# First attention of a two-layer network on one core: the order of an iteration's pieces, their PSUM places, the row sums and the kept queries are changed

## The reference, cut to what matters

```python
x = layer_norm(ctx); lat = layer_norm(layernorm(x))
q = lat @ Wq                                # 512 x 1024 for a batch
kv = concatenate([x, lat], axis=1) @ Wkv    # 32 + 512 keys and values
dots = einsum('bhid,bhjd->bhij', q, k) * scale
attn = softmax(dots, axis=-1)
out = einsum('bhij,bhjd->bhid', attn, v) ... @ Wout
x = x + out
# then: a routed feed-forward (8 experts, best one), a second attention over the
# context alone, and a second routed feed-forward (8 experts, best two)
```

## Time and profile before

| what | value |
|---|---|
| median of 3 runs | 803.49 us (798.53, 803.49, 803.7) |
| the profiled execution's own time | 803.94 us |
| its span, first to last instruction | 802.2 us |
| mean granted TensorE clock | 0.94 |
| PE busy | 705.0 us, 88% of the span, 4966 matmuls |
| PEld busy | 451.9 us, 56% |
| DVE busy | 473.4 us, 59% |
| ACT busy | 384.8 us, 48% |
| POOL busy | 378.6 us, 47% |
| chain that ended last | PE 74%, issue 8%, DVE 7%, ACT 4%, POOL 3%, DMA 2% |

### The profile page before, as it was taken

The page is one execution under the profiler, slowest core; times in us unless marked ns, Lnnn a source line. Parts: engine busy times, 40 slices in busy tenths (PEclk is TensorE's granted clock), DMA queues, the critical chain, the costliest instruction groups (busy, mean ns, idle before and its releaser), DMA issues.

```text
span 802.2 us, 14393 instructions
## 1 busy us (share of the span) xinstructions
PE 705.0 (88%) x4966; PEld 451.9 (56%) x4966; DVE 473.4 (59%) x950; ACT 384.8 (48%) x572; POOL 378.6 (47%) x369
## 2 busy tenths in 40 slices
PE   4999999999999999999999999986993777468871
PEld 4554555555555545555545455486993443458771
DVE  4646484595594875676675666653444287634443
ACT  4465554554654563654554643353661543235450
POOL 7164463563563574464365454524334126745542
PEclk9999999999999999999999999998997697569996
DMA  9999999950000000000030003302205200213215
GB/s 252 199 203 200 205 170 5 4 2 1 1 1 2 4 11 1 1 1 2 1 119 1 1 1 107 119 17 57 58 25 170 54 1 31 64 46 82 74 55 177
DMA packets 109869, 50.64 MB, mean 63 GB/s; under 512 B 44804, under 2 KB 103048, under 8 KB 109800
## 3 DMA queue, kind: packets, MB, share of 16 engines
q1 hardware_dynamic: 106280, 42.46, 35.7%
q0 software_dynamic: 3520, 7.27, 2.6%
HBM read 20.07 MB, written 29.64 MB: 62 GB/s over the span
## 4 chain that ended last, share of the span: by engine, by line
PE 74%; issue 8%; DVE 7%; ACT 4%; POOL 3%; DMA 2%; SPq 1%; another core or an unknown queue 1%; ACTq 0%; POOLq 0%; DVEq 0%
PE PSUM L1583 14%; PE PSUM L1615 13%; PE PSUM L1436 9%; PE PSUM L1550 5%; PE PSUM L1452 3%; PE PSUM L1681 3%; PE PSUM L1399 3%; PE PSUM L1400 3%; PE PSUM L1401 3%; PE PSUM L1564 2%; PE PSUM L1557 2%; PE PSUM L1601 2%; PE PSUM L1645 2%; PE PSUM L1395 1%; PE PSUM L1765 1%
## 5 line engine op out<-in xcount | busy, mean ns | idle before, releaser
L852 ACT ACTIVATE PT<-PSUM 128x1024 f32<-128x1024 f32 x128 | 128.6, 1024 | 133.8 <-PE PSUM L1583 133.5
L677 POOL TENSOR_TENSOR PSUMS<-PT 128x1024 f32<-128x1024 f32 x32 | 76.0, 2375 | 210.2 <-ACT PT L852 171.2
L1230 DVE TENSOR_REDUCE TOPS<-PSUM 128x2 f32<-128x1024 f32 x128 | 152.1, 1220 | 9.2 <-PE PSUM L1550 8.8
L677 POOL TENSOR_TENSOR PSUMS<-PSUMS,PT 128x1024 f32<-128x1024 f32 x62 | 149.6, 2413 | 16.8 <-ACT PT L852 9.8
L1615 PE MATMUL PSUM<-PT,BIG 128*64 128x512 f32 x512 | 130.6, 611 | 0.0
L1436 PE MATMUL PSUM<-XGT,WS 128*128 128x128 f32 x680 | 93.5, 289 | 19.9 <-ACT WS L769 17.3
L1436 PEld LDWEIGHTS PSUM<-XGT,WS 128*128 128x128 f32 x680 | 87.2, 204 | 22.1 <-DVE XGT L1178 19.6
L1186 DVE TENSOR_TENSOR SIL<-SIL,PSUM 128x256 f32<-128x256 f32 (+1 forms) x62 | 32.2, 519 | 76.7 <-ACT SIL L778 71.9
L778 ACT ACTIVATE SIL<-PSUM 128x256 f32<-128x256 f32 (+1 forms) x62 | 28.5, 459 | 73.9 <-PE PSUM L1436 56.9
L1220 DVE TENSOR_TENSOR KL<-PSUM,KH 128x512 fp32r<-128x512 f32 x32 | 22.1, 691 | 68.0 <-ACT KH L830 67.5
L1550 PE MATMUL PSUM<-KH,QH 64*128 64x512 f32 x256 | 58.6, 455 | 3.6 <-DVE QL L1223 3.6
(11 more groups left out here) (249 smaller groups left out, 1291.6 us busy)
## 6 DMA issues: line engine op xcount, KB each, us to landing
lists_d<-EMPTY SPq DMA_DIRECT2D x3, 2730.0 KB, 33.4
lists_b<-EMPTY SPq DMA_DIRECT2D x3, 2470.0 KB, 32.1
lists_d<-EMPTY SPq DMA_DIRECT2D x1, 2665.0 KB, 33.1
XG<-lists_d SPq DMA_DIRECT2D x39, 65.0 KB
lists_b<-EMPTY SPq DMA_DIRECT2D x1, 2405.0 KB, 17.1
BIG<-in_L_ffn_w SPq DMA_DIRECT2D x1, 2048.0 KB
W2ALL<-in_L_ffn_w SPq DMA_DIRECT2D x4, 512.0 KB, 5.4
PT<-results_d SPq DMA_DIRECT2D x8, 256.0 KB, 4.7
```

The lines of the kernel that those rows point to most:

```text
L677: pool.tensor_tensor(PSUMS[:, i % 2], PTT[:, i % 2, 0] if kt == 1 else PSUMS[:, i % 2], PTT[:, i % 2, kt], ALU.add).then_inc(s_ps, 1)
L852: act.activation(PTT[:, i % 2, kt], PSUM[:, place:place + 2, :], ACT.Exp, scale=DH ** -0.5).then_inc(s_exp, 1)
L1230: dve.tensor_reduce(TOPS[:, c, 0, :], PSUM[:, place:place + 2, :], AX.X, ALU.max).then_inc(s_max, 1)
```

## The change

The search's result is a new `ITERATION`, a table `WHERE` that says at which point of which iteration each of the slower-paced pieces stands, and a table `PLACE_AT` that gives most points a fixed place.

- In iteration i the four `t` and `s` pieces stand together (`s0 t1 s1 t2 t3 s2 t4 s3`), `p0 p1 p2` stand together after `qk` and `mt`, and `p3` stands before `s0`. The turning of the maxima moves to the next iteration: DVE's joining is now its own piece `mj` (`max_joined`) at the end, PE's and ACT's part stays `mt`, after the next `qk`.
- Banks 6 and 7 become a fourth place for `t2` and `s3`. `rows` therefore claims bank 7 each time, and its two halves are taken out separately: `sums_first` after the first (ACT copy, DVE add, 64 x 512 each), `sums_last` after the second (ACT copy, DVE add, and one more DVE add of two SBUF operands that joins the two). `rows` moves from the end of the iteration to the middle, between `t0` and `p3`.
- `one_low` is the subtraction that ended `one_over` part 3, now a piece of its own.
- There are five places for kept queries, `QF4` and `QF1`.
- In iteration 0 and in the last one the same points are used: values 2 and 3 of batch 0 follow `qk` of pair 1, the context values follow `t0`; the last group's `rest` gets `sums_last` and `one_low`.

The diff, without declarations and the moved `put` calls:

```diff
@@ -315,65 +317,70 @@
 
 
         ITERATION = (
-            "E A B PC CA0 C CA1 O0 ADD CS V qk p0 p1 t0 s0 t1 p2 t2 D s1 t3 p3 t4 P0 P2 s2 s3 rows mt O1 OUT "
-            "O2 O3").split()
+            "P0 SF A qk PC B mt p0 p1 p2 E t0 CS ADD RL V CA P2 R O rows C p3 s0 t1 s1 t2 t3 s2 t4 s3 mj D OUT").split()
+
+        PLACE_AT = dict(qk=1, mt=2, V=1, P0=2, P2=1, PC=0, OUT=1, C=(0, 0), B=0, CS=1, t0=2, t1=1, s0=2, t2=3, s1=0, t3=2, s2=1, t4=0,
+                        s3=3)
+
+        WHERE = dict(sums_first=(0, "CA"), sums_last=(0, "CS"), context_sums0=(0, "E"), context_sums1=(1, "CS"), context_add0=(0,
+                     "B"), context_add1=(1, "R"), one_over0=(1, "E"), one_over1=(1, "OUT"), one_over2=(2, "P0"), one_over3=(2,
+                     "E"), one_low=(2, "C"), spread0=(3, "P0"), spread2=(3, "B"), out=(3, "C"), add=(3, "C"), a_stats=(0, "SF"),
+                     a_rstd=(0, "PC"), a_out=(1, "CA"), a_turn=(2, "CS"), a_split=(3, "ADD"), values0=(4, "P0"), values1=(4, "PC"),
+                     values2=(4, "D"), values3=(5, "A"), r0_stats=(4, "P0"), r0_rstd=(4, "C"), r0_out=(5, "RL"), r0_turn=(6, "B"),
+                     r0_logits=(6, "RL"), r0_top=(7, "SF"), r0_hot=(7, "SF"), r0_run=(7, "RL"), r0_slot=(7, "V"), r0_send=(7,
+                     "OUT"))
 
         beside = [{} for _ in range(ALL + 1)]
 
         def put(i, at, name, a):
             beside[i].setdefault(at, []).append((name, a))
+
+        def put_at(step, base, name, a):
+            after, at = WHERE[step]
+            put(base + after, at, name, a)
         for g in range(2 * B):
-
-            put(GROUP * g + GROUP - 1, "CS", "context_scores", g)
-            for half in range(2 if g < 2 * B - 1 else 0):
-                put(GROUP * (g + 1) + 1, "PC", "context_sums", (g, half))
-                put(GROUP * (g + 1) + 1, f"CA{half}", "context_add", (g, half))
...
-                put(i + 6, "C", "r0_top", b - 1)
-                put(i + 7, "A", "r0_hot", b - 1)
-                put(i + 7, "D", "r0_run", b - 1)
+                for step in ("r0_stats", "r0_rstd", "r0_out", "r0_turn", "r0_logits", "r0_top", "r0_hot", "r0_run", "r0_slot", "r0_send"):
+                    put_at(step, i, step, b - 1)
 
         first_top = [("top", (0, c)) for c in range(TOPS_OF)]
         order = [("qk", 0), ("context_keys", 1)] + first_top[0:2] + [("values", (0, 0))] + first_top[2:4] + [("values", (0, 1))]
-        order += first_top[4:] + [("max_turn", 0), ("context_kept", 1), ("counters", 0)]
+        order += first_top[4:] + [("max_joined", 0), ("max_turn", 0), ("context_kept", 1), ("counters", 0)]
 
         instead = [[("values", (0, 2))], [], [("values", (0, 3))], [("context_values", 0), ("spread_rounded", 0)]]
+        placed = [None] * len(order)
         for i in range(ALL):
             for at in ITERATION:
+                before = len(order)
                 if at[0] == "s":
                     order.append(("scores", (i, int(at[1]))))
-                elif at in ("qk", "mt") and i + 1 < ALL:
-                    order.append(("qk" if at == "qk" else "max_turn", i + 1))
+                elif at in ("qk", "mj") and i + 1 < ALL:
+                    order.append(("qk" if at == "qk" else "max_joined", i + 1))
+                elif at == "mt":
+                    order += [("max_turn", i)] if i else []
                 elif at[0] == "t" and i + 1 < ALL:
                     order.append(("top", (i + 1, int(at[1]))))
                 elif at[0] == "p":
@@ -382,16 +389,19 @@
                     order.append(("rows", i - 1))
                 else:
                     order += beside[i].get(at, [])
+                where = PLACE_AT.get(at)
+                placed += [where[i % 2] if isinstance(where, tuple) else where] * (len(order) - before)
         last = 2 * B - 1
         for at in ITERATION:
             order += beside[ALL].get(at, [])
+        placed += [None] * (len(order) - len(placed))
 
 
 
         b = B - 1
         rest = [("e_tables", 0), ("kv_copies", 0), ("context_sums", (last, 0), 2, 2), ("rows", ALL - 1), ("context_add", (last, 0)),
-                ("one_over", (last, 0))] + [("pv", (ALL - 1, kt)) for kt in range(KT)]
-        rest += [("one_over", (last, c)) for c in range(1, 4)] + [("context_sums", (last, 1), 4, 2), ("context_add", (last, 1)),
+                ("sums_last", last), ("one_over", (last, 0))] + [("pv", (ALL - 1, kt)) for kt in range(KT)]
+        rest += [("one_over", (last, c)) for c in range(1, 4)] + [("one_low", last), ("context_sums", (last, 1), 4, 2), ("context_add", (last, 1)),
                  ("e_tables", 2), ("masks", 0)]
         rest += [("kv", 0), ("kv_kept", 0), ("spread", GROUP * last, 0, 2), ("spread", GROUP * last + 2, 4, 2), ("ex", 0), ("ex", 1),
                  ("ek", 0), ("ek", 1), ("e_tables", 3), ("out", last, 0, 1), ("add", last), ("ew", 0), ("ew", 1), ("eg", 0), ("r0_stats", b),
@@ -402,9 +412,9 @@
                  ("ev", 1), ("eg", 4), ("table", 4), ("ev", 2), ("table", 5), ("es", 4), ("ed", 3),
                  ("ev", 3), ("ed", 4), ("ev", 4)]
         order_a, place, out_at, sums_at = [], 0, {}, {}
-        for name, a in order:
-            order_a.append((name, a, 2 * (place % 3), 2))
-            place += name in TAKES_BANKS
+        for (name, a), at in zip(order, placed):
+            order_a.append((name, a, 2 * (place % 3 if at is None else at), 2))
+            place += name in TAKES_BANKS and at is None
             if name == "out":
...
@@ -419,6 +429,10 @@
 
         scored = [(name, a) for name, a, place, banks in order_a if name in ("scores", "context_scores")]
         SCORED = {step: i + 1 for i, step in enumerate(scored)}
+
+        def query(i):
+
+            return QF4[:, i % (GROUP + 1), :] if i % (GROUP + 1) < GROUP else QF1[:, :]
 
@@ -828,9 +842,9 @@
                         act.wait_ge(s_sc, scores_of(a - 2))
                     act.activation(QH[:, a % 2, :], PSUM[:, place, :], ACT.Copy).then_inc(s_qkh, 1)
                     act.activation(KH[:, a % 2, :], PSUM[:, place + 1, :], ACT.Copy).then_inc(s_qkh, 1)
-                    if a >= GROUP:
-                        act.wait_ge(s_sc, context_of(a // GROUP - 1))
-                    act.activation(QF[:, a % GROUP, :], PSUM[:, place, :], ACT.Copy).then_inc(s_qkh, 1)
+                    if a > GROUP:
+                        act.wait_ge(s_sc, context_of((a - 1) // GROUP - 1))
+                    act.activation(query(a), PSUM[:, place, :], ACT.Copy).then_inc(s_qkh, 1)
                 elif name == "max_turn":
@@ -863,11 +877,15 @@
                     if i >= OTS:
                         act.wait_ge(s_out, (i - OTS) // GROUP + 1)
                     act.activation(OT[:, i % OTS, :], PSUM[:, 6, :], ACT.Copy).then_inc(s_ot, 1)
-                elif name == "one_over" and a[1] == 0:
-                    g = a[0]
-                    act.wait_ge(s_rows, GROUP // 2 * (g + 1))
-                    if g:
-                        act.wait_ge(s_recl, g)
+                elif name == "sums_first":
+                    act.wait_ge(s_rows, GROUP // 2 * a + 1)
+                    if a:
+                        act.wait_ge(s_sums, a)
+                    act.activation(REC[64:128, :], PSUM[64:128, 7, :], ACT.Copy).then_inc(s_side, 1)
+                elif name == "sums_last":
+                    act.wait_ge(s_rows, GROUP // 2 * (a + 1))
+                    if a:
+                        act.wait_ge(s_recl, a)
                     act.activation(REC[0:64, :], PSUM[0:64, 7, :], ACT.Copy).then_inc(s_half, 1)
...
@@ -1232,7 +1250,7 @@
                         dve.tensor_reduce(TOPS[:, :, 1, :].rearrange("p t h -> p h t"),
                                           PSUM[:, place:place + 2, 0:TPB * M].rearrange("p h (t n) -> p h t n", t=TPB),
                                           AX.X, ALU.max).then_inc(s_max, 1)
-                elif name == "max_turn":
+                elif name == "max_joined":
                     dve.wait_ge(s_max, TOPS_OF * (a + 1))
                     if a:
                         dve.wait_ge(s_topt, a)
@@ -1244,16 +1262,26 @@
                     g, c = a
                     cols = slice(c * P, (c + 1) * P)
                     if c == 0:
-                        dve.wait_ge(s_half, g + 1)
-                        dve.tensor_tensor(REC[0:64, :], REC[0:64, :], PSUM[64:128, 7, :], ALU.add).then_inc(s_sums, 1)
                         dve.wait_ge(s_sums, g + 1)
                     dve.reciprocal(REC[0:64, cols], REC[0:64, cols]).then_inc(s_rec, 1)
-                    if c == 3:
-                        if g == 2 * B - 1:
-                            tables(0, True, "rows")
-                        dve.wait_ge(s_rech, g + 1)
-                        dve.wait_ge(s_rec, 4 * (g + 1))
-                        dve.tensor_tensor(RECS[64:128, :], REC[0:64, :], RECS[0:64, :].bitcast(F32), ALU.subtract).then_inc(s_recl, 1)
+                    if c == 3 and g == 2 * B - 1:
```

(45 more changed lines are left out.)

40 lines of the change are left out of this document (13 added, 27 removed).

## The result

The kernel after takes 810.35 us (809.07 to 811.75), the kernel before in the same comparison 801.97: 8.4 us more by these medians. The ratio estimated from all runs is 1.009, 95% interval 1.0053 to 1.0127. The forecast was 801.5 in a range of 792 to 810, so the time lies just above the range, and the change costs 0.9% where 0.2% of gain was forecast. Of all the runs here only this comparison was made on the first chip. On a second one, where what lies behind the attention takes some 23 us less (287.4 and 264.5 us behind `p3` of pair 31 in the two traces of the kernel after), it was 788.90 against 780.84, 1.0124 (1.0082 to 1.0167).

What follows compares the result with a forecast made beforehand. The prediction took PE to bound the attention stage (busy 468.1 of 472.0 us). Its terms, -2.4 - 6.5 - 2.5 + 3 + 0.4 + 2.4 + 3.6 = -2.0, against the median of 803.49 gave 801.5 us, range 792 to 810.

Steps and rivals of the forecast that it cites:

- `out` 6 and the turn of 31: Iteration 31: `out` waits 1.2 us for the routing counts' place, the maximum's turn 1.0 for the first `spread`'s.
- Pieces' order: The new order shortens each of 30 full iterations from 11.54 to 11.46 us: -2.4 us, bounds 0 and -7.8.
- companions: Pieces beside the iteration: `spread` and `values` move beside `qk`, with fewer changes of form: -2.5 us, bounds 0 and -4.
- QL: PE's waits from before vanish, as `t1` no longer shares a place with a `qk` whose QL is late: -6.5 us.
- fewer changes of form at the end: In the end's sum, fewer changes of matmul form give back 0.6 us.
- the predicted 0.43 for `s0`: Iteration 1 has nothing between `t0` and `p3`, so `s0` waits 0.45 us for its place: +0.4 us.
- `rows` for POOL: `rows`, now mid-iteration, waits for POOL's third addition: 0.63 to 0.95 in iterations 6 and 26, less in seven: +3 us.
- The slow rival: POOL's additions last 2.66 us instead of 2.38, hand-off long: `rows` waits 13.2 us instead of 3; 811.7 us, chance 0.09.
- The start: Iteration 0: values 3, context values and `s0` wait 1.3, 1.5 and 1.4 us for places: +2.4 us, bounds +1 and +3.5.
- The end: From iteration 31: waits of the turn, `out` and the last `rows`, plus one addition: +3.6 us, bounds +2 and +5.
- "right": Plain iteration near 11.9 us, no `t1` wait for QL, `rows` waiting in 6 and 26, `p0` near 48.9, `out` 6 waiting.
- "wrong": Signs against the forecast: an iteration at 11.3 us or below, or `rows` waiting in every second one.

Runs made afterwards that it cites:

- e2: Kernel before, with the second half of `context_sums` and its addition moved behind `qk`, seven times: 780.56 us, 1.0025 times before.
- e4: e1_pair, with the second half of `context_sums` reading the first half's rows, so both use the same row groups: 796.47 us, 1.0216 times before.
- e5: Kernel after, with `context_sums` halves of groups 0 to 6 adjacent again and other pieces' places held: 786.79 us, 1.0093 times before.
- e3: Kernel after, with values 3 and context values in other places in iteration 0, later rotating places shifting too: 796.31 us, 1.0203 times before.
- e6: Kernel after, with values 3 and context values in other places in iteration 0, all later pieces held: 783.09 us, 1.0031 times before.
- e8: e7 plus e6's start, other places in iteration 31 and the last `context_sums` halves adjacent: 777.14 us, 0.9960 times before.
- the repeat: Kernel after, unchanged, once more on a second chip: 788.90 us, 1.0124 times before.
- e10: e8 with the second half of the last `context_sums` back behind the reciprocals: 777.90 us, 0.9967 times before.
- e11: e10 with five instead of three idle matmuls in front of `spread` 28: 775.70 us, 0.9943 times before.
- e1_pair: Kernel after, with `context_sums` halves of groups 0 to 6 adjacent again, rotating places shifting too: 792.20 us, 1.0161 times before.
- e7: e5 with `s0` and `t3` in the first place, `s1` and `t4` in the third, some routing pieces moved: 782.03 us, 1.0016 times before.

## Why the prediction was wrong

*The step that failed: `context_sums`.* The forecast let "the same matmuls move", put the halves of `context_sums` apart and gave that move no cost. Every row needed was in the trace: 1.05 for sixteen matmuls in seven places, and 1.02 for the eight of the last group (510.33 to 511.35). That last one the prediction read as a slow hand-off from POOL, 0.47; it was PE still at work on its half. One row misread gave two errors: 7.4 us left out, and a hand-off that made `rows` too dear. That a half takes as long as the pair is shown by e2 (apart in before), e4 (same row groups) and e5 (together in after). It is PE's time. What the kernel loses by it is less: 1.2 us of the stretch in e5 and 2.8 in e2, since the halves stood where PE would have waited.

*Places of the routing.* Also missing, 3.9 us: the prediction walked `out` 6 and the turn of 31 (1.2 and 1.0 forecast, 1.3 and 1.1 found), but not the logits, the counts and the context scores, which rotate or stand behind DVE. e3 shows how much hangs on this: the same edit as e6 with the rotation moved on cost 10.8 us in the stretch.

*Pieces' order (-2.4), companions (-2.5), QL (-6.5), fewer changes of form at the end (-0.6).* Together -12.0 forecast, and 4.9 as large waits and 7.6 in the rest found, 12.5. That the sum fits is in part luck. Iteration 1 to 2 took 11.94 us (44.65 to 56.59), 11.9 announced, with the predicted 0.43 for `s0`. But without that wait it is 11.5, what it was before, against 11.46 announced: the bare order gave nothing. So the 7.6 must lie with the companions and the small waits, which I did not separate.

*`rows` for POOL (+3).* Mis-sized: two waits of 0.45 in iterations 6 and 26, nothing in the seven that have a piece ahead. The hand-off is smaller than both bounds, 0.15 and 0.47. By the rows it is 121.19 - (118.77 + 2.37) = 0.05, and it is so in all eighteen waits of this kind in four traces (after twice, e5, e8). POOL's ends are the least certain of the profile.

```profile
118.77 2.37 POOL L691 TENSOR_TENSOR PSUMS<-PSUMS,PT 128x1024 f32<-128x1024 f32 x1
...
121.19 1.07 PE L1670 MATMUL PSUM<-PSUMS,ROWS_F 128*32 128x512 f32 x8 [0.38 <-POOL PSUMS L691]
```

The slow rival hung on the long hand-off and on additions of 2.66 us. No addition of the kernel after lasted over 2.41.

*A row read wrong beside it.* The prediction says that DVE's subtraction of 1.05 us beside an addition shows less than a lock for the whole instruction. The rows show no less:

```profile
111.95 5.17 POOL L677 TENSOR_TENSOR PSUMS<-PSUMS,PT 128x1024 f32<-128x1024 f32 x2 [0.43 <-ACT PT L852]
113.83 1.06 DVE L1256 TENSOR_TENSOR RECS<-REC,RECS 64x512 fp32r<-64x512 f32 x1 [0.91 <-ACT RECS L877]
```

The first of the two additions took 2.40 and ended at 114.35. The subtraction began 0.52 before that and ended 0.55 after it, so it lasted 0.38 longer than the 0.68 of an undisturbed one. In all seven cases of this kind it ended 0.54 to 0.56 after the addition, and the next addition, begun meanwhile, took 2.63 to 2.66 instead of 2.38. So the subtraction met only the last half microsecond of the addition; that it waited that out, and the next addition waited for it, fits these rows. Nothing in the sum hangs on it.

*The start (+2.4).* All three waits were there (1.3, 1.5, 1.4), and without them (e6) the total is 5.8 us less, 4.1 of which the trace shows. From `qk` of pair 1 to `p0` of pair 0 it is 17.10 us before and 19.89 after: +2.8. The profiled execution hid this: its `context_keys` took 1.98 us instead of 2.59 and `qk` of pair 1 began 2.6 us sooner than before. In the repeat `context_keys` took 2.59 and `p0` of pair 0 started at 49.29, near the announced 48.9. That can be most of the difference between 5.2 us by the profiles and 8.4 by the medians; with one trace of each it is not shown.

*The end (+0.7 behind `p0` of pair 31).* `out` 7 came 0.44 later; the second addition took 0.69. The remaining 1.4 us of the 1.8 lie in the experts' part, which the change does not touch. From the first expert's matmuls to the end the twelve traces on the other chips have 248.8 (e3) to 255.5 us (e10) for the same code, 252.5 and 255.5 in e11 and e10, which differ by two idle matmuls. So 1.4 us between one trace and one trace says nothing of the change. Why this part varies: open.

*The signs.* Every sign that the prediction named for "right" came, and none for "wrong": they tested the terms that had been walked. The piece without a term had no sign.

## What to carry to other kernels

Before moving a piece apart from its neighbour, price it where it already stands alone: here matmuls on different row groups shared their time only while they followed each other. Price waits by walking each buffer, those that rotate too, and count what a piece covers before calling it a cost: some 7 us more of PE's time in `context_sums` were 1.2 us of the stretch in one kernel and 2.8 in another. When an experiment changes how many pieces rotate, pin all the others, or it measures the rotation. And before one trace is called better than another, look how far two traces of one kernel lie apart.

## What the runs showed of the hardware

Two sets of eight 32-row matmuls took 1.05 us together on four row groups, 1.02 each when apart, and 1.87 together on the same two groups.

A wait can be followed by a lower clock. In e1_pair PE waited 1.4 us for the place of the routing's logits from 372.6 on; the granted clock, 1.00 before, was then (stretch, busy us, clock third from the end):

```profile
374.00:376.00 2.00, 2.00 (x12) 1.47 (x16) 0.19 (x1) 0.00 (x0) 0.00 (x0) 0.63 0.04 8
376.00:378.00 2.00, 2.00 (x10) 0.30 (x4) 0.07 (x1) 0.59 (x1) 0.00 (x0) 0.50 0.00 0
378.00:380.00 2.00, 2.00 (x8) 0.83 (x6) 1.29 (x2) 0.60 (x1) 0.00 (x0) 0.50 0.01 4
```

`rows`, `p3`, `s0` there took 1.87, 1.91 and 1.87 us instead of 1.00, 1.01 and 1.03, 2.6 more in these three pieces; 0.50 is the lower of the two levels, 1.2 GHz. The clock fell in the same way after four waits of this size ahead of the logits, two in e1 and two in e4 (0.50 to 0.72 in stretches of 3 us). It stayed at 1.00 after the same wait in the kernel after (1.37 at 485), after ten waits of 1.3 to 1.5 in e3, two of them ahead of the same logits, and after the 2.5 us of e7. So the length of the wait alone does not decide; what does is open.
